# Talking heads: the scores of a later tile ahead of the mixing within a step

## The chip, the cores and the metric

The kernel runs on one core of one Trainium2 chip. The metric is the device time of one execution in microseconds. A NeuronCore has TensorE (PE in the profile, its weight loads PEld), VectorE (DVE), ScalarE (ACT), GpSimd (POOL) and SyncE (SP), which run their own instruction streams and meet at semaphores.

## The reference

The program is a small two-layer network over 16 images of 548 tokens (36 image patches and 512 text tokens) of width 192, all in float32: a patch embedding, a Performer attention, a gated attention, then an attention with talking heads, and a switched mixture of nine experts. The change lies in the attention with talking heads, which is, with 12 heads of 16 channels, for each image:

```python
attn = jnp.einsum('bhnd,bhmd->bhnm', q, k) * scale
attn = jnp.einsum('gh,bhnm->bgnm', th1_w, attn) + th1_b[None, :, None, None]
attn = jax.nn.softmax(attn, axis=-1)
attn = jnp.einsum('gh,bhnm->bgnm', th2_w, attn) + th2_b[None, :, None, None]
out = jnp.einsum('bhnm,bhmd->bhnd', attn, v)
```

So the scores of the heads are mixed once before the softmax and once after it, and the values are summed with the mixed probabilities.

## The kernel before

`build` (line 2750 on) runs the stages one after the other, with a barrier between them. `talking_heads` (line 1793 on) is the stage of the change. It cuts the 550 query rows of an image into 55 tiles of 10 queries (`NTILE`), so 16 images make 880 tiles. For tile n:

- **POOL** (L1937) multiplies the queries by the first mixing's weights into `qg`, so that the first mixing is part of the scores' matmul. `qg` has three slots.
- **TensorE, scores** (L2231): `qg` against the keys, 6 matmuls (12 records in the trace), 125 rows by 548 keys, into a pair of PSUM banks. They raise `score`.
- **DVE** (L2048, L2051): the row maximum from PSUM and the bias of the exponential (`bias`).
- **ACT, exponential** (L2140): from PSUM into `P`, with the row sums. Its second record, the read of the accumulator, ends it, and it raises `prob`.
- **DVE** (L2061, L2065): the reciprocal of the sums, and the second mixing's weights divided by them, `mixn` (`scaled`).
- **TensorE, mixing** (L2218): `P` against `mixn`, 10 matmuls (20 records), which normalises, mixes the heads and turns the tile, into banks 6 and 7. It raises `mixed`.
- **ACT, copy** (L2130): banks 6 and 7 into `P2` (`p2_in`). The next tile's mixing waits for it.
- **TensorE, values** (L2256): once per group of nine tiles (the last group has ten), at the group ends `ENDS` = 8, 17, 26, 35, 44 and 54: `P2` against the values, 120 records.

The order on each engine is written out by hand over `STEPS`, (b, i, n) with image b, tile i of the image and n = 55 b + i. TensorE in step n (L2209 on) mixes tile n, makes the scores of tile n + 3 (`SB` = 3), then does the step's *item*, if it has one, and the values at a group end. ACT in step n copies tile n out (waits for `mixed`) and then makes the exponential of tile n + 2; at a group end also that of n + 3, and none in the step after it. DVE in step n works on the maximum of tile n + 2 and the scaled weights of tile n + 1. POOL in step n makes `qg` of tile n + 4.

The items are the smaller matmuls of the neighbouring images, put into fixed steps by `SLOTS` (L1799): Y03 and Y4 (output projection, steps 3 and 8), Xb and Xa (turning the normalised tokens, 8 and 13), Ra and Rb (the same for the next stage, 17 and 22), Q0, Q1, Q2 (queries, 26, 31, 35), K01 and K2 (keys, 40 and 44), La and Lb (expert logits, 40 and 44), V4 and V03 (values' projection, 44 and 54). Y, R and L belong to the image before, the others to the image after. Five items (3, 13, 22, 31, 40) stand in steps without values, six (8, 17, 26, 35, 44, 54) in steps with them.

Banks 0 to 5 form three pairs. Every use (a tile's scores, an item, the values) takes the next pair in turn, in the order of the list `uses`, and `wait_bank` (L1872) makes TensorE wait until the use three before has been read out:

```python
for part, m in uses[u - SB] if u >= SB else ():
    if part == "T":
        eng.wait_ge(prob, m + 1)
    elif part == "Z":
        eng.wait_ge(summed, m + 1)
```

"T" is a tile, freed by its exponential, and "Z" the values. Between plain steps the use three before the scores of tile n + 3 is tile n. In the two steps after an item without values it is tile n + 1 (n being the step's own number); in the step after a group end it is tile n + 2; for an item it is tile n + 1, and for the values behind an item tile n + 2. The change leaves the list and all waits as they are.

Of the kernel before, what the change touches and what calls it, by code (L numbers as in the profile page):

```python
# [27 lines left out]
R = 110  # L28
T = 5
# [26 lines left out]
HQ = H * QH  # L56
MR = 64 + HQ + 1
SB = 3
# [6 lines left out]
MB = 6  # L65
# [1727 lines left out]
def talking_heads(k, A, logits, tokens, turned, wz, bz, xz):  # L1793
    nc, X, PS, ident = k.nc, k.X, k.PS, k.ident
# [9 lines left out]
    with ExitStack() as ctx:  # L1804
# [17 lines left out]
        mixn = sb("mixn", [MR, SB, H, QH])  # L1822
        P = sb("P", [MR, SB, NP])
# [3 lines left out]
        def sem(name):  # L1827
            return nc.alloc_semaphore("th_" + name)
# [5 lines left out]
        largest, bias, recip, scaled = sem("largest"), sem("bias"), sem("recip"), sem("scaled")  # L1834
# [34 lines left out]
        def is_tile(n):  # L1869
            return 0 <= n < NT  # L1870
# [19 lines left out]
        with nc.Block() as block:  # L1890
# [257 lines left out]
            @block.tensor  # L2148
            def _(pe):
                def turn(bank, part, im):  # L2150

                    if part[0] == "X":
                        pe.wait_ge(xn_in, T * im + (1 if part == "Xb" else T))
                    elif part == "Ra":
                        pe.wait_ge(ra_in, im + 1)
                    else:
                        pe.wait_ge(rn_in, im + 1)
                    for t in range(T - 1) if part[1] == "a" else (T - 1,):
                        for c in range(KC):
                            o, at = (bank + c, t * R) if t < T - 1 else (bank + 1, c * R)  # L2160
                            ins = pe.transpose(PS[0:C, o, at:at + R], xn[:, t, c * C:(c + 1) * C], ident[0:R, 0:R])
                    return ins

                def product(part, im, u):
                    bank = 2 * (u % SB)
                    if part[0] in "XR":
                        ins = turn(bank, part, im)
                    elif part[0] == "Y":
                        pe.wait_ge(summed, (im + 1) * GROUPS)
                        for t in range(4) if part == "Y03" else (4,):  # L2170
                            to = PS[0:R, bank + t // 2 % 2, t % 2 * D:(t % 2 + 1) * D]
                            for c in range(2):
                                ins = pe.matmul(to, oT[:, c, t * R:(t + 1) * R], wo[:, c, :], start=c == 0, stop=c == 1)
                    elif part[0] == "Q":
                        c = int(part[1])
                        pe.wait_ge(taken["X"], count("Xa", im))
                        for ci in range(KC):
                            for a in range(2):
                                ins = pe.matmul(PS[a * PC:(a + 1) * PC, bank + a, 0:HALF], wq[0:kin(ci), ci, c],
                                                xT[0:kin(ci), ci, a * HALF:(a + 1) * HALF], start=ci == 0, stop=ci == KC - 1)  # L2180
                    elif part[0] == "K":
                        for c in ((0, 1) if part == "K01" else (2,)):
                            for ci in range(KC):
                                for a in range(2):
                                    ins = pe.matmul(PS[a * PC:(a + 1) * PC, bank + c % 2, 0:HK], wk[0:kin(ci), ci, c * PC:(c + 1) * PC],
                                                    xT[0:kin(ci), ci, a * HK:(a + 1) * HK], start=ci == 0, stop=ci == KC - 1)
                    elif part[0] == "V":
                        for t in range(4) if part == "V03" else (4,):
                            to = PS[0:R, bank + t // 2 if t < 4 else bank + 1, t % 2 * D:(t % 2 + 1) * D]
                            for c in range(KC):  # L2190
                                ins = pe.matmul(to, xT[0:kin(c), c, t * R:(t + 1) * R], wv[0:kin(c), c, :],
                                                start=c == 0, stop=c == KC - 1)
                    else:
                        pe.wait_ge(taken["R"], count("Rb", im))
                        pe.wait_ge(ready, 2)
                        for t in range(3) if part == "La" else range(3, T):
                            for c in range(KC):
                                ins = pe.matmul(PS[0:R, bank, HK + t * E1:HK + (t + 1) * E1], rT[0:kin(c), c, t * R:(t + 1) * R],
                                                ws[0:kin(c), c, :], start=c == 0, stop=c == KC - 1)
                    ins.then_inc(done[part[0]], 1)  # L2200

                def stream(count):
                    for _ in range(count):
                        pe.matmul(PS[:, MB, 0:2 * D], ident[0:C, :], wk[0:C].rearrange("p c n -> p (c n)"), start=True, stop=True)

                TAIL = {"Y03": 4, "Ra": 7, "La": 1}
                stream(5)
                pe.wait_ge(ready, 1)
                for b, i, n in STEPS:  # L2209
                    if is_tile(n):  # L2210
                        p = n % SB
                        pe.wait_ge(scaled, n + 1)
                        if n:
                            pe.wait_ge(p2_in, n)
                        for t in range(T):
                            for s in range(2):
                                a = slice(64 * s, 64 * s + HQ + 1)
                                ins = pe.matmul(PS[0:R, MB + s, t * HQ:(t + 1) * HQ], P[a, p, t * R:(t + 1) * R], mixn[a, p],  # L2218
                                                start=True, stop=True)
                        ins.then_inc(mixed, 1)  # L2220
                    if is_tile(n + SB):
                        m = n + SB
                        p, bank, im = m % SB, 2 * (tile_at[m] % SB), m // NTILE
                        pe.wait_ge(qg_in, m + 1)
                        if m % NTILE == 0:
                            pe.wait_ge(taken["K"], count("K2", im))
                        wait_bank(pe, tile_at[m])
                        for c in range(NC):
                            for a in range(2):
                                s = slice(a * PC, (a + 1) * PC)  # L2230
                                ins = pe.matmul(PS[0:MR, bank + a, 0:HK], qg[s, p, c, 0:MR], kT[s, im % 2, c, :],  # L2231
                                                start=c == 0, stop=c == NC - 1)
                        ins.then_inc(score, 1)
                    if (b, i) in item_at:
                        wait_bank(pe, item_at[b, i])
                        for part, im in items(b, i):
                            if b == B and part in TAIL:
                                pe.wait_ge(p2_in, NT)
                                stream(TAIL[part])
                            product(part, im, item_at[b, i])  # L2240
                    if is_tile(n) and i in ENDS:
                        g = ENDS.index(i)
                        nq = GQ if g < NG else QL * QT
                        pe.wait_ge(p2_in, n + 1)
                        if g == 0:
                            pe.wait_ge(taken["V"], count("V03", b))
                        wait_bank(pe, values_at[b, i])
                        bank = 2 * (values_at[b, i] % SB)
                        for hg in range(HG):
                            for t in range(T):  # L2250
                                for j in range(4):
                                    if hg < 2:
                                        h, at, c = 2 * j + hg, (2 * j + hg) * 32 - hg * HD, 0
                                    else:
                                        h, at, c = 8 + j, (8 + j) * 32, 1
                                    ins = pe.matmul(PS[32 * j:32 * j + 32, bank, c * nq:(c + 1) * nq],  # L2256
                                                    v[:, b % 2, t].rearrange("p h d -> p (h d)")[:, at:at + 32], P2[:, t, h, 0:nq],
                                                    start=t == 0 and hg != 1, stop=t == T - 1 and hg != 0)
                        ins.then_inc(pv, 1)
                stream(6)  # L2260
# [549 lines left out]
```

## Time and profile before

| | |
|---|---|
| median of 3 runs | 4689.63 us (4688.78 to 4690.82) |
| profiled execution: time, span | 4690.51 us, 4688.7 us |
| mean granted TensorE clock | 0.991 |
| PE busy | 4554.5 us (97%) |
| DVE, ACT, POOL busy | 2549.3, 2183.1, 1671.0 us |
| instructions | 141401 |
| the stage of the talking heads | steps 0 to 879 from about 1338 to 3965 us |

The views are the page (busy time of each engine over the whole span), the busy times in a chosen stretch, and the instructions in order of time. In the last, a row is start, duration in us, engine, line, operation, what it writes and reads, and how many records are merged; a bracket gives the idle time of the engine before it and what ended that. A row of busy times in a stretch gives the stretch, its length, the busy us (and records) of PE, PEld, DVE, ACT and POOL, and then the granted TensorE clock, the DMA share and GB/s. A PE matmul may start before the one ahead has ended, since they are pipelined; clock 1.00 is 2.4 GHz and 0.50 is 1.2 GHz.

### The profile page before, as it was taken

The page shows a single profiled execution, that of the slowest core. Times are in us where ns is not written, and L with a number is a line of the kernel's source. Part 1 is how long each engine was busy: PE and PEld are TensorE (multiplying, and loading weights), DVE is VectorE, ACT ScalarE, POOL GpSimd, SP SyncE. Part 2 cuts the span into 40 slices and gives each one's busy share as a digit, 9 for nine tenths or more (in the row PEclk, how much of TensorE's full clock was granted, in tenths as well). Part 3 has the DMA queues.
Part 4 walks back from the last instruction along what each step waited for, and adds up shares of the span by engine and source line. Part 5 has one row for each costly group of instructions (what it writes and reads, how often), then busy time and mean ns, then how long its engine had stood idle before and what let it go on. Part 6 is the DMA issues. An engine that isn't in the chain of part 4 may idle for free. (4 is left out here: it accounts for less than half of the span.)

```text
span 4688.7 us, 141401 instructions
## 1 busy us (share of the span) xinstructions
PE 4554.5 (97%) x58206; PEld 3744.1 (80%) x58206; DVE 2549.3 (54%) x7440; ACT 2183.1 (47%) x5035; POOL 1671.0 (36%) x2777
## 2 busy tenths in 40 slices
PE   6999998999889999999999999999999999999998
PEld 4666665776678888888888888888888888899998
DVE  5667886666555555455555555555555544442333
ACT  3443443555545554554455455445545544212443
POOL 1103335777633333333333333333333333001555
PEclk8999999999999999999999999999999999999999
DMA  4112110000000000000000000000000000232333
GB/s 109 23 30 48 38 31 7 1 2 1 1 14 2 13 13 2 20 13 13 3 13 13 2 13 13 7 8 13 13 2 13 13 3 17 74 90 66 65 65 56
DMA packets 122476, 110.77 MB, mean 24 GB/s; under 512 B 63975, under 2 KB 110396, under 8 KB 121844
## 3 DMA queue, kind: packets, MB, share of 16 engines
q1 hardware_dynamic: 94447, 66.34, 6.1%
q0 software_dynamic: 16768, 23.59, 2.9%
q10 hardware_dynamic: 10628, 11.80, 1.1%
q8 instruction: 472, 7.73, 0.7%
q14 instruction: 161, 1.31, 0.1%
HBM read 59.76 MB, written 41.48 MB: 22 GB/s over the span
## 5 line engine op out<-in xcount | busy, mean ns | idle before, releaser
L1937 POOL TENSOR_TENSOR th_qg<-th_qT,w_th_th 128x180 f32<-128x180 f32 x1760 | 846.3, 503 | 1617.1 <-PE PS L2231 1607.5
L2231 PE MATMUL PS<-th_kT,th_qg 64*125 64x274 f32 x10560 | 1420.5, 400 | 0.0
L2130 ACT ACTIVATE th_P<-PS 110x600 f32<-110x600 f32 x880 | 647.0, 735 | 1119.1 <-PE PS L2218 1119.1
L2048 DVE TENSOR_REDUCE th_nmx<-PS 125x1 f32<-125x548 f32 x880 | 641.0, 728 | 902.8 <-PE PS L2231 902.8
L2218 PEld LDWEIGHTS PS<-th_mixn,th_P 61*110 61x110 f32 x17600 | 985.8, 173 | 96.0 <-issue 20.2
L2231 PEld LDWEIGHTS PS<-th_kT,th_qg 64*125 64x125 f32 x10560 | 947.5, 184 | 136.9 <-issue 0.2
L2218 PE MATMUL PS<-th_mixn,th_P 61*110 61x60 f32 x17600 | 980.2, 254 | 3.5 <-ACT th_P L2130 1.8
L2140 ACT ACTIVATE th_P<-PS,th_nb 125x548 f32<-125x548 f32 x880 | 621.0, 706 | 106.9 <-DVE th_nb L2051 106.9
L1370 POOL TENSOR_SCALAR ga_P<-ga_P,ga_rw 110x110 f32<-110x110 f32 (+4 forms) x240 | 264.9, 1115 | 160.3 <-DVE ga_rw L1538 159.5
L2051 DVE TENSOR_SCALAR th_nb<-th_nmx,w_th_b 125x1 f32<-125x1 f32 x880 | 240.1, 273 | 32.2
L2256 PEld LDWEIGHTS PS<-th_P,th_v 110*32 110x32 f32 x11520 | 229.7, 110 | 28.6 <-issue 27.5
L2256 PE MATMUL PS<-th_P,th_v 110*32 110x90 f32 (+1 forms) x11520 | 250.2, 244 | 2.1 <-issue 1.2
L2065 DVE TENSOR_SCALAR th_mixn<-w_th_mix,th_rs 125x60 f32<-125x60 f32 x880 | 225.0, 256 | 31.8
L2455 POOL DMA_INDIRECT ex_cx<-ex_tokens,ex_token_of x77 | 77.0, 1000 | 343.1 <-DVE ex_b L2629 250.7
L1021 PE MATMUL PS<-w_pf_wK,pf_xT 64*110 64x456 f32 x960 | 196.1, 555 | 1.4 <-ACT pf_xT L920 1.4
L1599 ACT ACTIVATE ga_PT<-PS 110x440 f32<-110x440 f32 (+3 forms) x240 | 102.3, 426 | 199.2 <-PE PS L1684 196.8
L2387 ACT ACTIVATE ez_h<-PS,ex_cb 128x128 f32<-128x128 f32 x462 | 127.5, 375 | 133.3 <-PE PS L2715 133.3
L2468 POOL DMA_INDIRECT out_h<-ex_cy,ex_token_of x77 | 132.9, 1726 | 136.5 <-DMA out_h<-ex_cy,ex_token_of 120.5
L2400 ACT ACTIVATE ez_h<-PS,ex_bz 128x550 f32<-128x550 f32 x96 | 68.9, 719 | 241.2 <-PE PS L2654 241.2
L2140 ACT ACTIVATION_READ_ACCUMULATOR th_P<-PS,th_nb 125x1 f32 x880 | 178.1, 202 | 0.0
L2715 PE MATMUL PS<-ex_cxT,ex_wz 64*128 64x128 f32 x2772 | 175.5, 278 | 0.3 <-ACT ex_cxT L2418 0.3
L2715 PEld LDWEIGHTS PS<-ex_cxT,ex_wz 64*128 64x128 f32 x2772 | 160.7, 188 | 13.4 <-issue 12.8
(364 smaller groups left out, 6407.3 us busy)
## 6 DMA issues: line engine op xcount, KB each, us to landing
pf_xT<-pf_spill SPq DMA_DIRECT2D x32, 412.5 KB, 5.4
ex_tokens<-th_xn SPq DMA_DIRECT2D x124, 82.5 KB
pf_spill<-pf_xT SPq DMA_DIRECT2D x16, 412.5 KB, 3.7
ex_turned<-th_rT SPq DMA_DIRECT2D x16, 412.5 KB, 3.1
ex_x<-ex_turned SPq DMA_DIRECT2D x32, 206.2 KB, 4.4
out_h<-X SPq DMA_DIRECT2D x16, 330.0 KB
ex_w<-in_L_ffn_W ACTq DMA_DIRECT2D x18, 288.0 KB
ex_w<-in_L_ffn_W ACTq DMA_DIRECT2D x8, 576.0 KB
```

The lines of the kernel that those rows point to most:

```text
L1021: ins = pe.matmul(PS[0:R, p + a, 0:HM + D], xT[half, slot(u), c, cols(u)], wK[half, c, :], start=c == 0, stop=c == NC - 1)
L1370: pool.tensor_scalar(P[:, n % 4, u, 0:keys(t)], P[:, n % 4, u, 0:keys(t)], rw[:, n % 4, u:u + 1], None, ALU.mult).then_inc(scaled, 1)
L1937: ins = pool.tensor_tensor(qg[:, m % SB, :, 64 * s:64 * s + HQ].rearrange("p c (h n) -> p c h n", n=QH), qT[:, im % 2, :, at + s * QH:at + ...
L2048: dve.tensor_reduce(nmx[:, p:p + 1], PS[0:MR, bank:bank + 2, 0:HK], AX.XY, ALU.max, negate=True) \
L2051: dve.tensor_scalar(nb[:, p:p + 1], nmx[:, p:p + 1], b1[:, 0:1], b1[:, 0:1], ALU.subtract, ALU.add) \
L2065: dve.tensor_scalar(mixn[:, p], mix[:], rs[:, p:p + 1], None, ALU.mult).then_inc(scaled, 1)
L2130: act.activation(P2[:, :, :, at * QT:(at + 1) * QT].rearrange("p t h (s n) -> p s (t h) n", s=2), PS[0:R, MB:MB + 2, 0:VO].rearrange("p s ...
L2140: act.activation(P[:, p, 0:N].rearrange("p (a n) -> p a n", a=2), PS[0:MR, bank:bank + 2, 0:HK], ACT.Exp, bias=nb[:, p:p + 1], accum_out=r ...
L2218: ins = pe.matmul(PS[0:R, MB + s, t * HQ:(t + 1) * HQ], P[a, p, t * R:(t + 1) * R], mixn[a, p], start=True, stop=True)
L2231: ins = pe.matmul(PS[0:MR, bank + a, 0:HK], qg[s, p, c, 0:MR], kT[s, im % 2, c, :], start=c == 0, stop=c == NC - 1)
L2256: ins = pe.matmul(PS[32 * j:32 * j + 32, bank, c * nq:(c + 1) * nq], v[:, b % 2, t].rearrange("p h d -> p (h d)")[:, at:at + 32], P2[:, t, ...
L2715: ins = pe.matmul(PS[:, 2 + 2 * (j % 2) + a, i * SL:(i + 1) * SL], cw[s, j % 2, c, i, :], cxT[s, j % 2, c, :], start=c == 0, stop=c == NC - 1)
```

## The change

Within each step of the loop on TensorE the block that makes the scores of tile n + 3 is moved ahead of the block that mixes tile n. Both blocks keep their matmuls, waits and semaphores.

```diff
--- before.py
+++ after.py
@@ -2207,17 +2207,6 @@
                 stream(5)
                 pe.wait_ge(ready, 1)
                 for b, i, n in STEPS:
-                    if is_tile(n):
-                        p = n % SB
-                        pe.wait_ge(scaled, n + 1)
-                        if n:
-                            pe.wait_ge(p2_in, n)
-                        for t in range(T):
-                            for s in range(2):
-                                a = slice(64 * s, 64 * s + HQ + 1)
-                                ins = pe.matmul(PS[0:R, MB + s, t * HQ:(t + 1) * HQ], P[a, p, t * R:(t + 1) * R], mixn[a, p],
-                                                start=True, stop=True)
-                        ins.then_inc(mixed, 1)
                     if is_tile(n + SB):
                         m = n + SB
                         p, bank, im = m % SB, 2 * (tile_at[m] % SB), m // NTILE
@@ -2231,6 +2220,17 @@
                                 ins = pe.matmul(PS[0:MR, bank + a, 0:HK], qg[s, p, c, 0:MR], kT[s, im % 2, c, :],
                                                 start=c == 0, stop=c == NC - 1)
                         ins.then_inc(score, 1)
+                    if is_tile(n):
+                        p = n % SB
+                        pe.wait_ge(scaled, n + 1)
+                        if n:
+                            pe.wait_ge(p2_in, n)
+                        for t in range(T):
+                            for s in range(2):
+                                a = slice(64 * s, 64 * s + HQ + 1)
+                                ins = pe.matmul(PS[0:R, MB + s, t * HQ:(t + 1) * HQ], P[a, p, t * R:(t + 1) * R], mixn[a, p],
+                                                start=True, stop=True)
+                        ins.then_inc(mixed, 1)
                     if (b, i) in item_at:
                         wait_bank(pe, item_at[b, i])
                         for part, im in items(b, i):
```

## Rows read from the trace of the kernel before

**Rows 1.** The page, busy time of each engine: us, share of the span, instructions.
```profile
PE 4554.5 (97%) x58206; PEld 3744.1 (80%) x58206; DVE 2549.3 (54%) x7440; ACT 2183.1 (47%) x5035; POOL 1671.0 (36%) x2777
```
**Rows 2.** Busy times in a stretch, the steps of the stage from 1338 us.
```profile
1338.00:3957.00 2619.00, 2615.95 (x41381) 2269.46 (x41383) 1382.79 (x4258) 1338.79 (x2811) 874.58 (x1778) 1.00 0.04 10
```
**Rows 3.** In order of time, a plain step and the start of the next.
```profile
2405.26 1.09 PE L2218 MATMUL PS<-th_mixn,th_P 61*110 61x60 f32 x20
...
2406.14 1.23 PEld L2231 LDWEIGHTS PS<-th_kT,th_qg 64*125 64x125 f32 x12
...
2406.24 0.27 DVE L2051 TENSOR_SCALAR th_nb<-th_nmx,w_th_b 125x1 f32<-125x1 f32 x1
2406.40 0.73 ACT L2130 ACTIVATE th_P<-PS 110x600 f32<-110x600 f32 x1 [1.63 <-PE PS L2218]
...
2406.62 0.25 DVE L2065 TENSOR_SCALAR th_mixn<-w_th_mix,th_rs 125x60 f32<-125x60 f32 x1
2407.01 0.70 ACT L2140 ACTIVATE th_P<-PS,th_nb 125x548 f32<-125x548 f32 x1
2407.40 1.18 PEld L2218 LDWEIGHTS PS<-th_mixn,th_P 61*110 61x110 f32 x20
2407.60 0.20 ACT L2140 ACTIVATION_READ_ACCUMULATOR th_P<-PS,th_nb 125x1 f32 x1
...
2408.50 1.23 PEld L2231 LDWEIGHTS PS<-th_kT,th_qg 64*125 64x125 f32 x12
```
**Rows 4.** In order of time, the last mixings of the stage.
```profile
3957.37 1.27 PE L2218 MATMUL PS<-th_mixn,th_P 61*110 61x60 f32 x20
...
3958.68 0.73 ACT L2130 ACTIVATE th_P<-PS 110x600 f32<-110x600 f32 x1 [0.95 <-PE PS L2218]
...
3959.52 1.07 PEld L2218 LDWEIGHTS PS<-th_mixn,th_P 61*110 61x110 f32 x20 [1.02 <-DVE th_mixn L2065]
...
3961.64 2.06 PE L2218 MATMUL PS<-th_mixn,th_P 61*110 61x60 f32 x20 [0.91 <-ACT th_P L2130]
```
**Rows 5.** In order of time, TensorE, item Q1 and the mixing behind it.
```profile
2414.83 1.15 PE L2179 MATMUL PS<-th_xT,w_th_wq 96*64 96x275 f32 x8
...
2415.91 1.18 PE L2218 MATMUL PS<-th_mixn,th_P 61*110 61x60 f32 x20
```
**Rows 6.** In order of time, TensorE: V03, Y03, Y4, values, Xa, Rb, K01, K2, V4.
```profile
2317.87 2.87 PE L2191 MATMUL PS<-w_th_wv,th_xT 96*110 96x192 f32 x16
...
2333.04 2.85 PE L2173 MATMUL PS<-w_th_wo,th_oT 128*110 128x192 f32 x16
...
2347.85 0.90 PE L2173 MATMUL PS<-w_th_wo,th_oT 128*110 128x192 f32 x4
...
2348.87 2.54 PE L2256 MATMUL PS<-th_P,th_v 110*32 110x90 f32 x120
...
2363.36 0.96 PE L2161 MATMUL PS<-ident,th_xn 110*96 110x110 f32 x8
...
2389.28 0.39 PE L2161 MATMUL PS<-ident,th_xn 110*96 110x110 f32 x2
...
2441.51 2.07 PE L2185 MATMUL PS<-th_xT,w_th_wk 96*64 96x274 f32 x16
...
2454.43 1.15 PE L2185 MATMUL PS<-th_xT,w_th_wk 96*64 96x274 f32 x8
...
2456.30 0.88 PE L2191 MATMUL PS<-w_th_wv,th_xT 96*110 96x192 f32 x4
```
**Rows 7.** Busy times in stretches: two gaps that kept the clock, one that didn't.
```profile
379.20:382.60 3.40, 1.61 (x12) 0.92 (x12) 1.42 (x3) 0.86 (x2) 1.13 (x5) 1.00 0.00 0
1306.40:1309.60 3.20, 1.68 (x7) 0.93 (x6) 1.86 (x9) 0.00 (x0) 1.01 (x1) 1.00 0.00 0
1309.60:1313.00 3.40, 3.40 (x7) 1.69 (x6) 1.98 (x7) 0.00 (x0) 2.41 (x3) 0.50 0.98 224
3994.80:3998.20 3.40, 1.67 (x14) 1.27 (x14) 3.26 (x5) 2.47 (x3) 0.00 (x0) 1.00 0.88 340
```

## The prediction

> **What bounds the kernel now.** Read first the page's busy times, then the stretch of the talking heads alone, then single steps in order of time. TensorE is busy for 97% of the span [rows 1]; from 1338 to 3957 us, where the 880 steps of this change lie, it is busy for 2615.95 of 2619.00 us at a granted clock of 1.00 [rows 2]. So this phase has 3.05 us of TensorE idle time in all: no wait can be shortened to any profit, and whatever new wait the other order makes TensorE sit through is added to the end almost in full.
>
> A plain step (no item, no values) lasts 2.36 us: the scores' weight loads begin at 2406.14 and again at 2408.50 [rows 3]. Call E the end of a tile's mixing on TensorE: 2405.26 + 1.09 = 2406.35. ScalarE copies the mixed tile out from 2406.40, 0.05 us after E, starts the exponential of the tile two further on at 2407.01, and reads its sum out at 2407.60 for 0.20, so that the exponential is finished at 2407.80: **E + 1.45**. How fast TensorE resumes after ScalarE is seen only at the end of the phase: the copy ends at 3958.68 + 0.73 = 3959.41 and the next weight load starts at 3959.52, 0.11 us later [rows 4]. So TensorE can go on with what waits for that exponential at E + 1.56.
>
> **The change part by part.** Nothing is added or removed: matmuls, copies, DMAs and semaphore counts are the same, and no instruction of another engine, SP's and POOL's queues included, changes its place in its own queue. In plain steps the cyclic order (scores, mixing, scores, mixing) is the same too. What changes is which mixing stands ahead of which scores, and where the item and the values stand: before, mix(n), score(n+3), item, values; after, score(n+3), mix(n), item, values. I go through the waits.
>
> *POOL's products.* score(n+3) needs POOL's product, which POOL may write from score(n) on; that is three scores apart in both orders. Nothing.
>
> *Mixing.* It waits for DVE's scaled weights. These are ready at 2406.62 + 0.25 = 2406.87, and the weight load that needs them starts at 2407.40 [rows 3]: 0.53 us in hand, which the change lengthens by one score. It gains nothing, since nothing is lost there now.
>
> *Plain score.* score(n+3) takes the banks of tile n, whose exponential ScalarE makes in step n-2, behind the copy of tile n-2. Before, mix(n-1), mix(n) and two scores lie between mix(n-2) and it; after, mix(n-1) and one score. The time from E(n-2) to the load is then 2408.50 - 2406.35 = 2.15 us, against 1.56 needed: 0.59 us in hand. Nothing, but narrow. DVE's bias is no obstacle: it is ready at 2406.24 + 0.27 = 2406.51, 0.50 us ahead of its exponential [rows 3], and comes one score earlier after the change.
>
> *Score after an item.* The three bank pairs go round over tiles, items and values alike. When an item in step j (3, 13, 22, 31 or 40, those without values) has taken one, score(j+4) and score(j+5) get the banks of tiles j+2 and j+3, whose exponentials ScalarE makes in steps j and j+1. Before, a further score and mixing covered them. After, score(j+5) follows mix(j+1) directly, and mix(j+1) is what the copy and then that exponential wait for. Unhindered the load would start at 2406.14, 0.21 us ahead of E; now it starts at E + 1.56: **1.77 us** each, nothing beside it. For score(j+4) the item lies between. An item starts about 0.07 us ahead of the end of what precedes it and takes its busy time less 0.07: Q1 is busy 1.15 us and 1.08 us later the mixing starts [rows 5]. So the stall is 1.63 less the item's length L. From [rows 6], L is 2.78 (Y03), 0.89 (Xa), 0.32 (Rb), 1.08 (Q1), 2.00 (K01 alone): stalls of 0, 0.74, 1.31, 0.55 and 0, together 2.60 us per image.
>
> *Values.* At the six group ends (8, 17, 26, 35, 44, 54) the values take the bank of tile n+2, whose exponential follows the copy of tile n. Before, score(n+3) and the item stood between mix(n) and the values, now only the item. Stall again 1.63 - L: Y4 with Xb 1.02 (2347.85 to 2348.87 [rows 6]), Ra as Xa 0.89, Q0 and Q2 1.08 each, K2 with V4 at least 1.89, V03 2.80. That is 0.61 + 0.74 + 0.55 + 0.55 + 0 + 0 = 2.45 us. The score after the values needs the exponential of tile n+3, made next and 0.9 us later (0.70 + 0.20), at about E + 2.46; the values begin at E + 1.56 at the earliest and last over 2 us. Nothing.
>
> Sum per image: 5 x 1.77 + 2.60 + 2.45 = 13.90 us, for 16 images 222 us. The first image lacks the Y, R and L items and the last the X, Q, K and V ones. This removes four full stalls and their partners and leaves some values uncovered (1.63 instead of 0.55 to 0.74 us, or instead of nothing): about -3 us. At the end a score no longer separates two mixings, +1 us. **The stalls sum to 220 us.**
>
> *The clock.* 76 stretches of 1.56 us without work come into a phase that had none. The trace has nine TensorE gaps of 1.47 to 2.67 us that begin at full clock, from 379.2 to 3994.8 us. Six pass without loss, the first and last among them; after or within three (near 731.6, 758.4 and 1306.4 us) the clock goes to 0.50, its level of 1.2 GHz instead of 2.4 [rows 7]. At the phase's end, after two gaps and a mixing between them, a mixing takes 2.06 instead of 1.09 us [rows 4]. Bounds: no gap loses it (0), or every one does. A slow spell is at least the 3.4 us from 1309.6 [rows 7] and loses half of that, 1.7 us; for 76 this is 129 us. I take the share of the nine, a third, with this shortest spell, since steps without stalls follow each gap: 76 / 3 x 1.7 = 43 us.
>
> The Trainium skill, page "TensorE: Matmul & The Clock Gate", section "HAM oscillation — how this bites in real kernels", says that idle gaps between bursts can throttle the array again at every burst. By it the clock's term would be the 129 us, not 43; the rows show both outcomes.
>
> **Sum.** The profiled execution took 4690.51 us (span 4688.7 and 1.8 around it), 0.9 above the median of 4689.63. 4690.5 + 220 + 43 = 4953.5, less 0.9: **4953 us**.
>
> **Rivals.**
> *The clock holds.* The stalls are as above, and work on both sides of each gap keeps the clock; six gaps of nine speak for it, the slow mixing at the end against. 4690 + 220 = 4910 us.
> *Every full gap loses the clock.* This is the skill's warning as a mechanism of this kernel: mixings, scores of 1.6 us and gaps take turns. 4910 + 129 = 5039 us; it needs what only three gaps of nine did.
> *The bank waits do not bind; not slower.* If ScalarE's copy and exponential were done by the time TensorE reaches score(j+5), that is if the chain of 1.56 us after E were hidden as it is now, only the seams would be left. After an item or values the mixing starts with its loads uncovered and takes 1.18 instead of 1.09 us [rows 3, 5]; with a score there instead, up to 0.09 x 176 seams = 16 us would go, and of the 3 us idle some: 4672 us at best. It decides at a chain of about 0: any copy and exponential after the mixing's end is longer, so it needs that the slot count above is wrong.
> *The change does nothing.* Plain steps keep their cyclic order; if the displaced seams cancel, 4690 us. Against it speaks the same count.
> *Small term.* If ScalarE's chain hides 0.3 us more than I read at each of the 76 full stalls and some 100 partial ones, the stalls are 170 and the time about 4860 with the clock held.
>
> **How the numbers follow.** Forecast (stalls and some lost clock, roughly 4925 to 5010) 0.50; clock holds 0.28; every gap loses it 0.08; smaller stalls 0.07; change does nothing 0.03; not slower through the seams 0.04, of which 0.01 is within 0.2%. A measurement of this kernel can tell about 0.2% (9 us) from no change. Chances: faster 0.03, same 0.04, slower 0.93. The range from 4885 to 5015 takes in the clock-holds case with a stall 0.15 us shorter each (176 x 0.15 = 26), and two lost clocks of three (86 us) with some us over; about 0.2 is left out.
>
> **What the changed profile would show.** In plain steps still 2.36 us from score to score. In steps j+1 and j+2 after an item without values, the score's first load idle until ScalarE's exponential, 1.56 us in step j+2; together some 155 us idle ahead of the scores. Ahead of the values some 37 us idle on the exponential or the copy, at group ends 0, 1, 2 and 3, not at 4 and 5. TensorE's idle time in the phase about 195 us instead of 3, its clock about 0.98 to 0.99 there, in short spells of 0.50. DVE and POOL as long as before. I am wrong if plain steps grow (then the 0.59 us in hand was misread), if the scores after items do not wait, if the stalls differ from 1.56, or if slow spells are absent or longer than the 3.4 us.

## The result, and the profile after

The changed kernel takes 4993.15 us (median of 3, 4985.00 to 5006.59) against 4689.63: a ratio of 1.0651, 95% interval 1.0622 to 1.068. It is slower by 304 us where 263 were forecast. The profiled execution took 5006.59 us, its span is 5004.8 us.

First the page, busy times as in [rows 1] and the costliest group; then the stage as in [rows 2]. TensorE's line numbers have changed places: L2220 is now the scores and L2231 the mixing.

```profile
PE 4664.5 (93%) x58206; PEld 3911.7 (78%) x58206; DVE 2645.7 (53%) x7440; ACT 2168.0 (43%) x5035; POOL 1667.2 (33%) x2777
...
L2220 PE MATMUL PS<-th_kT,th_qg 64*125 64x274 f32 x10560 | 1496.2, 414 | 165.0 <-ACT th_P L2140 160.8
```
```profile
1338.00:4270.00 2932.00, 2721.84 (x41372) 2433.34 (x41371) 1478.79 (x4256) 1322.60 (x2808) 874.82 (x1778) 0.97 0.04 9
```

TensorE's idle time in the stage has gone from 3 us to 210 us (about 195 forecast), and its clock from 1.00 to 0.97 (0.98 to 0.99 forecast). The waits of TensorE in the stage (line, what it waited for, us in total, times, longest) say where:

```profile
PE PS L2220 <- ACT th_P L2140: 160.8, 123, 1.6
PE PS L2256 <- ACT th_P L2140: 37.4, 62, 1.3
```

Scores and values wait for the exponential, as the prediction had it (about 155 and 37 us). Around one full gap, two tiles after item Y03, in order of time:

```profile
2447.36 1.09 PE L2231 MATMUL PS<-th_mixn,th_P 61*110 61x60 f32 x20
...
2448.49 0.73 ACT L2130 ACTIVATE th_P<-PS 110x600 f32<-110x600 f32 x1 [3.89 <-PE PS L2231]
2449.12 0.71 ACT L2140 ACTIVATE th_P<-PS,th_nb 125x548 f32<-125x548 f32 x1
2449.71 0.20 ACT L2140 ACTIVATION_READ_ACCUMULATOR th_P<-PS,th_nb 125x1 f32 x1
...
2450.06 2.23 PE L2220 MATMUL PS<-th_kT,th_qg 64*125 64x274 f32 x12 [1.61 <-ACT th_P L2140]
...
2452.01 2.06 PE L2231 MATMUL PS<-th_mixn,th_P 61*110 61x60 f32 x20
...
2453.79 3.13 PE L2220 MATMUL PS<-th_kT,th_qg 64*125 64x274 f32 x12
```

The mixing ends at 2448.45 and the exponential at 2449.91, E + 1.46; TensorE then sits idle for 1.61 us. From the start of the mixing to that of the scores it is 2.70 us, in a plain step of the same trace 0.92 to 0.93 (2417.47 to 2418.39), so the stall is 1.77 us. Then comes what the clock takes: the scores last 2.23 and 3.13 us where they take 1.61 at full clock, the mixing 2.06 instead of 1.09. The clock of a stretch just there is 0.50:

```profile
2452.00:2455.40 3.40, 3.40 (x30) 3.23 (x28) 1.00 (x2) 1.30 (x3) 1.79 (x4) 0.50 0.00 0
```

**Two parts of the time.** Span times mean clock is the span as it would be with no cycle withheld. Before it is 4688.7 x 0.991 = 4646.5 us; the rest, 42.2 us, was withheld. Of the three runs after (spans 5004.8, 4983.1, 4991.4; clocks 0.972, 0.976, 0.977) this makes 218, 217 and 230 us of stalls more than before, and 98, 77 and 73 us of clock; the clock's third digit is worth 2.5 us either way. Below, "stalls" and "clock" are these two differences to before, as means over the runs of a kernel.

### The profile page after: what moved, and what is told of

It is laid out like the page before. It is cut to its first block and busy times, and to the rows that moved or that the text cites. A ratio compares the mean times of both kernels' runs of the same rounds, so it can differ in the third digit from the quotient of the medians.

```text
span 5004.8 us, 141401 instructions
## 1 busy us (share of the span) xinstructions
PE 4664.5 (93%) x58206; PEld 3911.7 (78%) x58206; DVE 2645.7 (53%) x7440; ACT 2168.0 (43%) x5035; POOL 1667.2 (33%) x2777
## 5 line engine op out<-in xcount | busy, mean ns | idle before, releaser
L2220 PE MATMUL PS<-th_kT,th_qg 64*125 64x274 f32 x10560 | 1496.2, 414 | 165.0 <-ACT th_P L2140 160.8
L2220 PEld LDWEIGHTS PS<-th_kT,th_qg 64*125 64x125 f32 x10560 | 1021.5, 190 | 316.2 <-issue 170.7
L2231 PEld LDWEIGHTS PS<-th_mixn,th_P 61*110 61x110 f32 x17600 | 1061.7, 179 | 71.0 <-issue 3.1
L2231 PE MATMUL PS<-th_mixn,th_P 61*110 61x60 f32 x17600 | 1011.0, 258 | 2.7 <-ACT th_P L2130 2.7
L2061 DVE RECIPROCAL th_rs<-th_rs 125x1 f32<-125x1 f32 x880 | 142.6, 162 | 675.2 <-ACT th_P L2140 673.7
L2065 DVE TENSOR_SCALAR th_mixn<-w_th_mix,th_rs 125x60 f32<-125x60 f32 x880 | 297.8, 338 | 33.2 <-DVE th_rs L2061 2.7
L2256 PE MATMUL PS<-th_P,th_v 110*32 110x90 f32 (+1 forms) x11520 | 250.6, 244 | 45.9 <-ACT th_P L2140 37.4
```

The lines of the kernel that those rows point to most:

```text
L2065: dve.tensor_scalar(mixn[:, p], mix[:], rs[:, p:p + 1], None, ALU.mult).then_inc(scaled, 1)
```

## The experiments

**ScalarE's order.** In step n ScalarE copies tile n out, which waits for its mixing, and then makes the exponential of tile n + 2, which doesn't need that mixing. The experiments put this exponential first, everywhere or in chosen steps (`ahead` is the list of tiles whose exponential belongs to the step, `exponential(m)` the old instruction put into a function):

```diff
+                    early = n >= 1 and (CONDITION) and n + 2 in ahead
+                    if early:
+                        exponential(n + 2)
                     if is_tile(n):
...
-                    for m in filter(is_tile, ahead):
+                    for m in ahead:
+                        if not (early and m == n + 2):
+                            exponential(m)
```

`exp_first_all`, CONDITION `True`:

> The changed kernel, but ScalarE makes the exponential of tile n+2 ahead of the copy of tile n in every step. Theory (the stalls are the chain mixing, copy, exponential, bank): the exponential no longer waits for the mixing, all three kinds of stall vanish and the clock holds; about 4690 us, within 0.3% of the kernel before, TensorE idle in the stage under 10 us. Rival (the bank round trip itself is too long in the new order, whatever ScalarE does first): stays near 4990 us.

`exp_first_step2`, `(i - 1) in (3, 13, 22, 31, 40)`:

> The changed kernel, with the exponential ahead of the copy only in the step after an item without values (76 places), so that only the full stalls of 1.77 us go. Theory: 76 x 1.77 = 134 us of stalls go, and nearly all of the clock's loss (about 95 us) with them, since the gaps left are 0.6 to 1.3 us: about 4765 to 4780 us. Rival (the clock is lost at short gaps too): 4800 us or more. Rival (all stalls have one cause elsewhere, so that removing them in one place moves them on): less than 100 us gained.

`exp_first_rest`, `i in (3, 13, 22, 31, 40) or i in ENDS`:

> The changed kernel, with the exponential ahead of the copy only in the steps that have an item or end a group: the partial stalls ahead of the first score after an item (2.60 us per image) and ahead of the values (2.45 us) go, the full ones stay. Theory: 81 us less than the changed kernel, about 4912 us, with the clock's loss of about 95 us left. Rival (the clock's loss hangs on all gaps together): 4870 us or less.

| | median us | ratio, 95% | stalls | clock | waits for the exponential: scores; values |
|---|---|---|---|---|---|
| changed | 4993.2 | 1.0622 to 1.068 | 222 | 83 | 160.8; 37.4 |
| exp_first_all | 4684.6 | 0.9981 to 1.0 | -5 | -1 | 1.6; none |
| exp_first_step2 | 4789.9 | 1.0201 to 1.0236 | 92 | 8 | 40.2; 37.7 |
| exp_first_rest | 4837.3 | 1.0296 to 1.033 | 135 | 11 | 122.8; none |

(The last column is from the waits of each profile, us.) The chain is shown: with the exponential out from behind the copy all stalls are gone, with the change in place. This is how the first wait of the list reads with the full gaps alone and with the partial ones alone; the exponential is at L2129 in these kernels:

```profile
PE PS L2228 <- ACT th_P L2129: 122.8, 77, 1.6
```
```profile
PE PS L2228 <- ACT th_P L2129: 40.2, 47, 1.6
PE PS L2264 <- ACT th_P L2129: 37.7, 62, 1.3
```

The stalls add up: 135 + 92 = 227 against 222. The full ones are 135 us where 76 x 1.77 = 134 was expected. The partial ones and those ahead of the values, left by `exp_first_step2`, are 92 us where 81 were expected, so it came out some 10 us above its 4765 to 4780. The clock does not add up: 11 + 8 against 83. `exp_first_rest` came out 75 us under the 4912 expected, on the side of its rival.

**Work in the gap.** `fill_gap` puts two matmuls, whose result nobody reads, ahead of the scores two steps after an item:

```diff
+                        if n > 0 and (i - 2) in (3, 13, 22, 31, 40):
+                            fill(2, m + 1)
...
+                    wait_bank(pe, tile_at[m])
+                    for _ in range(count):
+                        pe.matmul(PS[:, 2 * (tile_at[m] % SB), 0:2 * D], ident[0:C, :], wk[0:C].rearrange("p c n -> p (c n)"), start=True, stop=True)
```

> The changed kernel, with two extra matmuls of 0.71 us each put into each full gap of 1.56 us, into banks that are free, so that TensorE waits as before but doesn't rest. They add 1.42 us of work where 1.56 us were idle. Theory (220 us are stalls, the other 80 to 95 us are the clock): the clock holds at the full gaps and the time is about 4905 to 4915 us, with the granted clock back near 0.99. Rival (the clock is not it, the stalls are some 300 us): 4990 us or more.

It took 4947.6 us (ratio 1.0533 to 1.0569): stalls 239, clock 18. In order of time a filled gap (mixing L2240, the added matmuls L2211, scores L2229) shows the stall unchanged, 2.70 us from mixing to scores, and the scores behind it at full clock:

```profile
2467.65 1.12 PE L2240 MATMUL PS<-th_mixn,th_P 61*110 61x60 f32 x20
2468.70 1.56 PE L2211 MATMUL PS<-w_th_wk,ident 96*128 96x384 f32 x4
2470.35 1.66 PE L2229 MATMUL PS<-th_kT,th_qg 64*125 64x274 f32 x12
```

So idling costs the clock, waiting alone doesn't: 65 us of 83 came back. The kernel holds its own control. None of the 76 filled gaps is followed by a slow spell. But the edit also fills at the four places in the first and the last image where the item is missing and the changed kernel has no gap. There the added matmuls had to wait for the exponential, and TensorE idled for 1.5 us each time:

```profile
PE PS L2211 <- ACT th_P L2140: 6.0, 4, 1.5
```

Three of these four are followed by a slow spell. The time missed the 4905 to 4915 because some 17 us more of stalls are in it. These four places are most of that: from mixing to scores it is 4.08 us there (4151.51 to 4155.58) instead of 0.92, 3.16 more, which makes 13 us. Where the rest lies is not shown.

```profile
4151.51 1.09 PE L2240 MATMUL PS<-th_mixn,th_P 61*110 61x60 f32 x20
4154.10 1.56 PE L2211 MATMUL PS<-w_th_wk,ident 96*128 96x384 f32 x4 [1.50 <-ACT th_P L2140]
4155.58 1.66 PE L2229 MATMUL PS<-th_kT,th_qg 64*125 64x274 f32 x12
```

**Which gaps cost the clock.** I took the non-additive result for a matter of neighbours: a partial gap one tile ahead of a full one. `exp_first_item3` has CONDITION `i in (13, 22, 31)`, `exp_first_ends` has `i in ENDS`.

> The changed kernel, with the exponential ahead of the copy only in the steps of Xa, Rb and Q1 (13, 22, 31): only the partial stall ahead of the first score after these items goes, one step ahead of a full stall that stays. Theory (the clock is lost above all where a partial gap stands one tile ahead of a full one, since full gaps alone lost 14 us): stalls fall by 42 us and the clock's loss from 92 us to some 15 to 25, so the span falls from some 5000 us to about 4885 us. Rival (all gaps add up to the clock's loss, the values' too): about 4920 us or more.

> The changed kernel, with the exponential ahead of the copy only at the group ends: only the stalls ahead of the values go. Theory: these gaps stand far from the full ones and cost the clock little; 42 us less than the changed kernel, about 4950 us. Rival (the clock's loss hangs on all gaps): 4910 us or less.

The first took 4942.9 us (1.0504 to 1.0593; stalls 188, clock 46, 57, 72 and 107 in its four runs), the second 4949.7 us (1.0527 to 1.0559; stalls 172, clock 86). The stalls fell roughly as expected (222 less 34 and less 50, where 42 each were forecast); the theory of neighbours fell, for the clock's loss stayed when they went. In the profile of `exp_first_item3` a slow spell follows 24 of the full gaps, in that of `exp_first_rest` 6, though on TensorE the instructions right around them are the same. That left the moment at which a gap falls. `rest_shifted` is `exp_first_rest` with the scores of one tile per image made twice, and `all_shifted` the same on `exp_first_all`:

```diff
-                        for c in range(NC):
+                        for c in [*range(NC)] * (2 if i == 49 else 1):
```

> The kernel of exp_first_rest (only the full gaps left), where TensorE makes the scores of one tile of each image (step 49) twice, 1.39 us more of dense work per image, far from every gap. Theory (whether a full gap costs the clock hangs on the moment at which it falls, and in exp_first_rest the moments repeated from image to image and happened to be good ones): the added work shifts the gaps against each other, 20 to 35 of the 76 lose the clock, 40 to 90 us; with 22 us of added work the time is 4895 to 4950 us. Rival (what counts is the work around a gap, and gaps with no other gap near them keep the clock): 4837 + 22 = 4859 us, within 8.

> Control: exp_first_all (no gap left) with the same scores made twice, 16 x 1.39 = 22 us more work and no clock to lose: 4707 to 4710 us. If it is further off, the added work costs something that rest_shifted must not be charged for.

`all_shifted` took 4708.5 us (1.0022 to 1.005), 24 above `exp_first_all` where 22 us of work were added: the added work is charged at its price. `rest_shifted` took 4896.2 us (1.0427 to 1.0461), 37 above what its rival allowed: stalls and added work 154, clock 51 (41 to 61) instead of 11. Sixteen of its full gaps are followed by a slow spell (20 to 35 were expected). Eleven of them come two tiles after Y03, out of 15 such gaps; in `exp_first_rest` none of these 15 had one. So whether a gap of 1.6 us costs the clock depends on when it comes, and where images repeat at an even pace it is the same items' gaps that are lucky again and again. `exp_first_rest` had luck. What makes a moment a bad one these runs don't settle, nor whether all of the distance from 51 us to the 70 and 86 of the two kernels that kept some partial gaps is luck.

One rival is left by the times: the kernels that lost little clock (`exp_first_step2`, `exp_first_rest`, `fill_gap`) were all run on one chip, the later ones on others. The profiles speak against a chip that spares short gaps. The gap of 1.3 us behind item Rb was followed by a slow spell 3 times of 15 in `exp_first_step2` and in `fill_gap`, 4 of 15 in the changed kernel and 6 of 15 in `exp_first_ends`, and three of the four gaps of 1.5 us in `fill_gap` were.

**ScalarE's order alone.** The kernel before with the exponential first, and the repetition beside it:

> The kernel before, with the exponential ahead of the copy in every step. Control: the order of scores and mixing is the old one. Theory: TensorE bound at its own work either way, no wait to lose, 4688 us within 0.1%. Rival (the 4 us that the changed kernel with this order was ahead come from ScalarE's order): 4684 us here too.

> The changed kernel with the exponential ahead of the copy in every step, again, beside the control. Theory (4 us of the seams: after an item or values a score stands where a mixing began with its loads uncovered): 4684 to 4686 us. Rival (no difference): 4688 us.

`changed_exp_first` took 4687.9 us (0.9984 to 1.0002), so its lead over the kernel before is not clear of no difference. `before_exp_first` took 4869.0 us (1.0366 to 1.0395), stalls 181, clock -2, a miss of both theories. Its steps in order of time (mixing L2226, scores L2239, exponential L2129, copy L2145):

```profile
2420.58 1.09 PE L2226 MATMUL PS<-th_mixn,th_P 61*110 61x60 f32 x20
...
2421.50 1.61 PE L2239 MATMUL PS<-th_kT,th_qg 64*125 64x274 f32 x12
2421.56 0.27 DVE L2051 TENSOR_SCALAR th_nb<-th_nmx,w_th_b 125x1 f32<-125x1 f32 x1
...
2421.87 0.72 ACT L2129 ACTIVATE th_P<-PS,th_nb 125x548 f32<-125x548 f32 x1 [1.78 <-DVE th_nb L2051]
...
2422.57 0.72 ACT L2145 ACTIVATE th_P<-PS 110x600 f32<-110x600 f32 x1
...
2423.44 1.18 PE L2226 MATMUL PS<-th_mixn,th_P 61*110 61x60 f32 x20 [0.33 <-ACT th_P L2145]
```

The mixing ended at 2421.67, but ScalarE now holds the copy back behind an exponential whose bias DVE has only just made from the last scores (ready at 2421.83); the copy ends at 2423.29, and the next mixing, which waits for it, comes 2.86 us after the last instead of 2.37. This happens in about every second plain step, and the steps between take 2.43 us; TensorE waits for the copy 307 times in this kernel, 93 us in all, and part of the rest of the 181 us is in matmuls that take longer, such as this mixing with 1.18 us for 1.09. With scores first that bias is a score and a mixing older when ScalarE wants it:

```profile
2365.82 0.20 ACT L2129 ACTIVATION_READ_ACCUMULATOR th_P<-PS,th_nb 125x1 f32 x1
...
2366.94 0.74 ACT L2145 ACTIVATE th_P<-PS 110x600 f32<-110x600 f32 x1 [0.93 <-PE PS L2239]
```

This is `exp_first_all` (mixing L2239): the exponential has been over for 0.92 us when the copy starts. Each of the two orders on TensorE has its own order on ScalarE; either one alone changed costs 179 or 304 us, both together nothing.

**The slack in plain steps.** One more ScalarE instruction between copy and exponential, in the changed kernel and in the one before:

```diff
+                        act.activation(pad[:, n % 4], ident[:], ACT.Copy)
```

> The changed kernel with one more ScalarE instruction (128 x 128, some 0.3 us) between the copy and the exponential of every step. Theory: plain steps keep 2.36 us, since 0.59 us are in hand there; the 76 full, some 46 partial and some 64 values' stalls grow by it each: 186 x 0.3 = 56 us, and somewhat more clock is lost: about 5050 to 5080 us. Rival (plain steps have no slack left): 694 plain steps grow too, over 5150 us.

> The kernel before with the same added instruction. Theory: the chain of copy and exponential is covered by a score and a mixing more, so nothing shows: 4688 us within 0.2%. Rival (ScalarE's time is near the bound in the old order too): 20 us or more above.

`pad_changed` took 5066.4 us (1.0791 to 1.0827): stalls 260, clock 117. The instruction delays the exponential by 0.20 us (a full gap is 1.78 us instead of 1.58), and 186 places x 0.20 = 37 us is what the stalls grew by (39). Plain steps did not grow. The time lies in the expected 5050 to 5080 partly by luck, since 56 us of stalls were expected and the clock made up for them with 35 us more. `pad_before` took 4691.8 us (0.9996 to 1.0015): there the chain is covered.

## Why the prediction was right

**Plain steps, POOL, mixing.** Right: their intervals in the timeline are 2.36 to 2.37 us as before, and with 0.20 us more on ScalarE still so.

**Score after an item.** Right: 76 full stalls forecast at 1.77 us, 134 us; the kernel that has only these has 135. TensorE idles for 1.59 to 1.61 us in them where 1.56 was forecast. The partial ones stand in the trace where they were placed.

**Values.** Right in place (62 waits, none behind K2 or V03 while an image follows), a little low in size: forecast 39 us in 16 images. The waits for the exponential there are 37.4 us, but 50 us went when `exp_first_ends` took them away.

**Sum of the stalls.** 220 forecast, 222 measured (217 to 230 in the three runs).

**The clock.** The mechanism was right, the term too small: 43 us forecast, 73 to 98 measured. Of its two factors the share of full gaps came out near (a third; 30 of 76 in the profile, with 5 more after partial gaps), and that is partly luck, since other kernels with the same 76 gaps lost 6, 16 and 24. The price was wrong: "with this shortest spell" took 1.7 us each, but 14 of the 36 spells lasted 6.8 us or more, and on average one cost 2.7 us. That is one of the prediction's own signs of being wrong, slow spells longer than 3.4 us. The reason given, that steps without stalls follow, did not hold the spells to their shortest. This is the 40 us by which the forecast was low.

The trace of before held the warning. Of the spells after its three gaps [rows 7] shows the shortest; the other two, as busy times in stretches, lasted 10.2 and 6.8 us:

```profile
732.70:742.90 10.20, 7.98 (x14) 4.61 (x15) 5.15 (x28) 0.00 (x0) 4.42 (x5) 0.50 0.19 45
760.00:766.80 6.80, 5.41 (x12) 4.07 (x13) 2.78 (x14) 0.92 (x3) 2.60 (x3) 0.50 0.02 2
```

With the mean of the three, 6.8 us, and so a price of 3.4 us, the same sum gives 76 / 3 x 3.4 = 86 us.

The rival in which every full gap loses, at 5039 us, was 46 us too high, and the one without a loss, at 4910, 83 us too low. The prediction took the first for the warning of the Trainium skill (page "TensorE: Matmul & The Clock Gate", section "HAM oscillation — how this bites in real kernels"). That section's gaps are waits for DMA of about 3 to 5 us, so it says nothing of every gap of 1.6 us, and its case is no support for the 129 us.

**The rival by which nothing is lost** rested on the chain being hidden; `exp_first_all` makes it so and gives 4684.6 and 4687.9 us in two sets. The 16 us that the seams could have brought are not there: after an item the scores take 1.66 instead of 1.61 us, so they too seem to start uncovered.

## What to carry to other kernels

When two blocks on a bound engine change places, list for each ring of buffers which use freed the slot and behind what that release is queued on the other engine; a slot that is a ring's length away in plain steps may be one step nearer where something irregular has taken a turn. An order on one engine and the order on its partner are one decision, so try them together. And price an idle gap on TensorE twice, as a stall and as a chance of some microseconds at half clock.

## What the runs showed of the hardware

Gaps of 1.6 us with the same instructions around them lost the clock or kept it, depending on when they came: 6 of 76 in one kernel, 16 when 1.39 us of work per image were added elsewhere, 24 in `exp_first_item3`, 30 in `exp_first_ends` and in the changed kernel. Where one fell, it was 1.6 to 2.7 us after TensorE had gone idle. In the changed kernel gaps of 1.3 us were followed by a fall in 4 of 15 cases, those of 0.5 to 1.1 us in 1 of 103. The slow spells lasted 3.4 or 6.8 us, rarely more. The same kernel differed by 55 us from run to run (`exp_first_item3`, 4926.5 to 4981.2), and that is clock: its stalls were 184 to 191 us in all four, its clock term 46 to 107.
